# Sorting edges on one core: one-hots and halves of the sort's moves dealt out differently to VectorE and ScalarE, seven matrix-product tiles placed ahead of the first move

## The reference, cut to what matters

```python
def _L0_gnn_ref(vertex_features, edge_index, w0, w1):
    w0_features = vertex_features @ w0
    w1_features = vertex_features @ w1
    dst, src = (edge_index[0], edge_index[1])
    messages = w1_features[src]
    neighbours = jax.ops.segment_sum(messages, dst, num_segments=vertex_features.shape[0])
    return jax.nn.relu(w0_features + neighbours)
...
edge_index = jnp.stack([src, dst])
x = _layernorm(x + _L0_gnn_ref(x, edge_index, L0_gnn_w0, L0_gnn_w1), axis=-1)
x = _layernorm(x + _L1_gnn_ref(x, L1_gnn_W, L1_gnn_attn_src, L1_gnn_attn_dst, edge_index, edge_type_8), axis=-1)
```

## Time and profile before

| | |
|---|---|
| median of 3 runs | 2756.26 us (2753.54 to 2758.73) |
| the profiled execution | 2753.3 us, span 2751.5 us |
| PE busy | 2293.7 us (83%) |
| VectorE busy | 1939.8 us (70%) |
| GpSimd busy | 1849.2 us (67%) |
| ScalarE busy | 1639.8 us (60%) |

### The profile page before, as it was taken

The page is one execution under the profiler, slowest core; times in us unless marked ns, Lnnn a source line. Parts: engine busy times, 40 slices in busy tenths (PEclk is TensorE's granted clock), DMA queues, the critical chain, the costliest instruction groups (busy, mean ns, idle before and its releaser), DMA issues.

```text
span 2751.5 us, 38106 instructions
## 1 busy us (share of the span) xinstructions
PE 2293.7 (83%) x9936; PEld 1659.4 (60%) x9936; DVE 1939.8 (70%) x4273; ACT 1639.8 (60%) x3465; POOL 1849.2 (67%) x1875
## 2 busy tenths in 40 slices
PE   7787798999999999999997677777778777777775
PEld 3455676777777776777764555565556555555541
DVE  8896666555555555555553688888888888888887
ACT  4563564666666666666654566666666666666643
POOL 1002677777777777777753777777777777777745
PEclk9897899999999999999997688888878887888888
DMA  5202355754544444444454544554455445544435
GB/s 153 67 22 90 117 150 137 228 179 151 167 149 153 159 152 161 154 160 143 155 127 163 138 138 138 147 141 138 138 142 146 138 138 148 139 138 138 142 92 159
DMA packets 177777, 387.53 MB, mean 141 GB/s; under 512 B 42669, under 2 KB 106867, under 8 KB 171042
## 3 DMA queue, kind: packets, MB, share of 16 engines
q0 software_dynamic: 83888, 233.09, 30.1%
q1 hardware_dynamic: 86626, 99.05, 12.3%
q10 hardware_dynamic: 7056, 52.99, 4.9%
HBM read 302.96 MB, written 82.03 MB: 140 GB/s over the span
## 4 chain that ended last, share of the span: by engine, by line
PE 49%; DVE 17%; POOL 13%; issue 12%; DMA 6%; DVEq 2%; ACT 1%; SPq 0%; POOLq 0%; ACTq 0%; PEldq 0%
PE ps L1687 21%; PE ps L1804 10%; PE ps L1739 10%; POOL region L1348 7%; POOL region L1303 5%; DVE nodes L895 4%; DMA region<-ha_d,idx_t 3%; PE ps L1787 2%; DVE region L884 2%; DMA region<-y_d,edge_z 2%; PE ps L1656 2%; DVE nodes L777 1%; PE ps L1644 1%; PE ps L1821 1%; DMA ha_d<-region 1%
## 5 line engine op out<-in xcount | busy, mean ns | idle before, releaser
L1303 POOL DMA_INDIRECT region<-y_d,edge_z x856 | 879.1, 1027 | 466.3 <-issue 240.3
L1348 POOL DMA_INDIRECT region<-ha_d,idx_t x880 | 896.0, 1018 | 306.9 <-issue 246.9
L777 DVE TENSOR_TENSOR nodes<-ps,nodes 128x512 f32 x856 | 592.0, 692 | 508.5 <-PE ps L1687 389.4
L1687 PE MATMUL ps<-region 128*128 128x256 f32 x3424 | 802.0, 388 | 66.3 <-DMA region<-y_d,edge_z 36.1
L1687 PEld LDWEIGHTS ps<-region 128*128 128x128 f32 x3424 | 657.8, 194 | 229.0 <-issue 109.3
L1804 PE MATMUL ps<-region 128*128 128x264 f32 x1760 | 618.6, 483 | 123.6 <-DVE nodes L895 119.3
L1804 PEld LDWEIGHTS ps<-region 128*128 128x128 f32 x1760 | 357.1, 229 | 300.0 <-DVE nodes L895 219.8
L895 DVE TENSOR_TENSOR nodes<-ps,nodes 128x264 f32 x880 | 373.5, 424 | 99.0 <-DVE nodes L895 48.6
L1461 ACT ACTIVATE region<-iota_n,edge_z 128x256 f32<-128x256 f32 x856 | 364.7, 499 | 62.7 <-PE ps L1687 56.5
L1739 PE MATMUL ps<-region,edge_z 128*128 128x512 f32 x784 | 359.9, 592 | 5.5 <-ACT region L1503 4.3
L1556 ACT ACTIVATE region<-region,ones 128x512 f32<-128x512 f32 x220 | 158.8, 722 | 270.2 <-PE ps L1804 264.9
(11 more groups left out here) (265 smaller groups left out, 1860.0 us busy)
## 6 DMA issues: line engine op xcount, KB each, us to landing
ha_d<-region ACTq DMA_DIRECT2D x49, 1056.0 KB, 4.8
region<-near_d SPq DMA_DIRECT2D x55, 512.0 KB, 5.4
region<-ha_d,idx_t POOLq DMA_INDIRECT x880, 4.1
region<-y_d,edge_z POOLq DMA_INDIRECT x856
edge_z<-level_d SPq DMA_DIRECT2D x55, 136.0 KB, 4.0
kl_d<-region SPq DMA_DIRECT2D x8, 903.0 KB, 9.8
edge_z<-kl_d SPq DMA_DIRECT2D x55, 129.0 KB
y_d<-edge_z SPq DMA_DIRECT2D x25, 256.0 KB, 3.2
```

What stands on the lines that cost most here:

```text
L777: v.tensor_tensor(into, ps[:, u, :], into, ALU.add).then_inc(added0, 1)
L1303: g.indirect_dma_start(rows0[c % RING][:, u, :], None, y_d, bass.IndirectOffsetOnAxis(ap=y_idx[:, k:k + 1], axis=0), bounds_check=node_bou ...
L1348: g.indirect_dma_start(rows[s][:, k, :], None, ha_rows, bass.IndirectOffsetOnAxis(ap=idx_t[:, B * b + k:B * b + k + 1], axis=0), bounds_ch ...
L1687: mm = t.matmul(ps[:, u, h * D:(h + 1) * D], lhsT=sel0[c % SEL][:, u, h * P:(h + 1) * P], rhs=rows0[c % RING][:, u, :], start=True, stop=True)
```

## The change

DVE now makes all the windows, also those of moves 0, 4, ..., 28, and no longer makes the halves. It makes the column one-hots of even moves only. ACT makes the halves, in eight instructions for each move (2 sides by 4, 104x64 elements each, a Copy with a scale that is read from `sides`), and the column one-hots of odd moves, as two Abs of 104x856 and one Relu of 104x1712. The pairs of buffers for the columns become three: even moves share one, moves 1, 5, 9, ... and 3, 7, 11, ... have one each; `columns_of(k)` on DVE still waits for `settle(k - 2)`. The ACT copy of the window numbers (`w_f`) is gone. Tiles 41 to 47 of y stand between the turning of `q_row` and the first move, with `columns_of(1)` on ACT after the copy of tile 44; tiles 48 and 49 follow moves 3 and 7.

```diff
 # constants and buffers
-    GOES_AT, Q_AT = 35, 40
+    GOES_AT, Q_AT, GAP = 35, 40, 7
-        S_c = [[view16(region, COLS * n + COLS // 2 * s, COLS) for s in range(2)] for n in range(2)]
+        S_both = [view16(region, at, 2, COLS) for at in (0, COLS, 9 * KR)]
+        S_c = [S_both[0], S_both[1], S_both[0], S_both[2]]
...
         def on_scalar(k):
-            return k % 4 == 0
+            return k % 2 == 1
         def y_tile_at(k):
-            return Q_AT + k // 2 + 1 if k % 2 and Q_AT + k // 2 + 1 < NT else None
+            tile = Q_AT + GAP + k // 4 + 1
+            return tile if k % 4 == 3 and tile < NT else None
...
 # VectorE
             places_of(0)
+            windows_of(0)
             for k in range(NBT):
                 values_of(k)
                 if k + 1 < NBT:
                     places_of(k + 1)
-                if k + 1 < NBT and not on_scalar(k + 1):
+                if k + 1 < NBT:
                     windows_of(k + 1)
-                columns_of(k)
-                if k:
-                    halves_of(k - 1)
+                if not on_scalar(k):
+                    columns_of(k)
...
 # ScalarE
+            def columns_of(k):
+                if k >= 5:
+                    a.wait_ge(o_ps, k - 3)
+                for s in range(2):
+                    last = a.activation(S_c[k % 4][0:WW, s, :], iota_h[0:WW, :], ACT.Abs,
+                                        bias=goes_col[0:WW, PP * (2 * k + s):PP * (2 * k + s) + 1], scale=-1.0)
+                last.then_inc(s_near, 1)
+                near_turns[0] += 1
+                a.wait_ge(s_near, near_turns[0])
+                a.activation(S_c[k % 4][0:WW, :, :], S_c[k % 4][0:WW, :, :], ACT.Relu, bias=ones[0:WW, 0:1],
+                             scale=-1.0).then_inc(cols_a, 1)
+
+            def halves_of(k):
+                a.wait_ge(moved, k + 1)
+                if k >= 2:
+                    a.wait_ge(o_ps, k - 1)
+                for s in range(2):
+                    for h in range(SIDES):
+                        last = a.activation(halves[k % 2][0:WW, s, :, h * HC:(h + 1) * HC],
+                                            ps[0:WW, 2 + k % 2, s * 2 * HC:(s + 1) * 2 * HC].rearrange("p (a n) -> p a n", a=2),
+                                            ACT.Copy, scale=sides[0:WW, 2 * k + s, 0, h:h + 1])
+                last.then_inc(halves_made, 1)
+
+            for tile in range(Q_AT + 1, Q_AT + GAP + 1):
+                keep_products(tile)
+                if tile == Q_AT + 4:
+                    columns_of(1)
             for k in range(NBT):
-                ahead = k // 4 * 4 + 4
-                if ahead < NBT:
-                    windows_of(ahead, TBG // 2 * (k % 4), TBG // 2 * (k % 4) + TBG // 2)
+                halves_of(k)
+                if k and k + 1 < NBT and on_scalar(k + 1):
+                    columns_of(k + 1)
                 if y_tile_at(k) is not None:
                     keep_products(y_tile_at(k))
...
 # TensorE
             turn_rows(q_row, 6).then_inc(sort_ps, 1)
+            for tile in range(Q_AT + 1, Q_AT + GAP + 1):
+                products(tile)
```

More of the change, by code:

```diff
@@ L81, in graph_layers @@
     EARLY = 6
-    GOES_AT, Q_AT = 35, 40
+    GOES_AT, Q_AT, GAP = 35, 40, 7
     assert WW <= P and COLS <= KR and OH <= 512 and E <= P * KR and NP_ * 512 < 2 ** 24
     assert WW * HC < HIGH and HIGH * HIGH <= 2 ** 24 and KR < HIGH and NPAIR <= 16
-    assert OH % 4 == 0 and OH <= 512 and NT - 1 - Q_AT <= NBT // 2 and 2 * NBT * PP <= P
+    assert OH % 4 == 0 and OH <= 512 and 0 <= NT - 1 - Q_AT - GAP <= NBT // 4 and 2 * NBT * PP <= P
     def dram(name, shape, dt):
@@ L197, in graph_layers @@
         q_i = view(region, 9 * KR, KR).bitcast(I32)
-        w_f = view(region, 10 * KR, KR)
         masks = [view(region, GA + KR // 2 * t, KR // 2).bitcast(BF16) for t in range(NPAIR)]
@@ L201, in graph_layers @@
         assert GA + NPAIR * KR // 2 <= RW - COLS
-        win = [view16(region, GA, TB, WW)] + [view16(region, GA + TB * WW // 2 * n, TB // 2, WW, 2) for n in range(1, 4)]
+        win = [view16(region, GA + TB * WW // 2 * n, TB // 2, WW, 2) for n in range(4)]
         at = [view16(region, GA + 2 * TB * WW + TB * HC * n, 2, TB // 2, HC, 2) for n in range(3)]
@@ L338, in graph_layers @@
         (pads_set, edges_in, acol_in, w_in, iotas, setup, sort_ps, sort_in, y_ps, y_done, y_kept, bt_made, masked,
-         counted, v_made, goes_made, cells_made, scans, summed, wp_made, split_made, grids_made, at_made, at_filled, win_v, win_a, moved,
+         counted, v_made, goes_made, cells_made, scans, summed, wp_made, split_made, grids_made, at_made, at_filled, win_v, cols_a, moved,
          halves_made, s_near, s_made, o_ps, y_ready, segs0, sel0_near, sel0_made, added0, pool_turns, rows_stored,
@@ L366, in graph_layers @@
         PS = {"counts": 1, "v": 2, "goes": 3, "q": 4, "bucket": 5, "wab": 6}
-        IN = {"v": 2, "goes": 3, "q": 5, "w_f": 6, "bucket": 8, "cells": 8, "wab": 11}
+        IN = {"v": 2, "goes": 3, "q": 5, "bucket": 7, "cells": 7, "wab": 10}
         def in_pairs(eng, first, end, body):
@@ L616, in columns_of @@
                 for s in range(2):
[L617 removed]
+                    v.tensor_scalar(S_c[k % 4][0:WW, s, :], iota_h[0:WW, :], goes_col[0:WW, PP * (2 * k + s):PP * (2 * k + s) + 1],
                                     None, ALU.is_equal).then_inc(s_made, 1)
[L620 to L629 removed]
             places_of(0)
+            windows_of(0)
             for k in range(NBT):
@@ L1421, in _ @@
             a.wait_ge(wp_made, 2)
-            a.copy(w_f, w_i).then_inc(sort_in, 1)
-            a.wait_ge(sort_in, IN["w_f"])
-            def windows_of(k, first, end):
-                if k >= 4 and first == 0:
-                    a.wait_ge(moved, k - 3)
-                to = win[k % 4]
-                for j in range(first, end):
-                    last = a.activation(to[:, j, :], iota_row[:, 0:WW], ACT.Abs, bias=w_f[:, TB * k + j:TB * k + j + 1],
-                                        scale=-1.0)
-                if end == TB:
-                    last.then_inc(s_near, 1)
-                    near_turns[0] += 1
-                    a.wait_ge(s_near, near_turns[0])
-                    a.activation(to, to, ACT.Relu, bias=ones[:, 0:1], scale=-1.0).then_inc(win_a, 1)
@@ L1633, in _ @@
             turn_rows(q_row, 6).then_inc(sort_ps, 1)
+            for tile in range(Q_AT + 1, Q_AT + GAP + 1):
+                products(tile)
             def move(k):
                 t.wait_ge(at_filled, 2 * k + 2)
-                window_ready(t, k)
+                t.wait_ge(win_v, k + 1)
                 if k >= 2:
@@ L1644, in move @@
                     mm = t.matmul(ps[0:WW, 2 + k % 2, j // TBG * 2 * HC:j // TBG * 2 * HC + 2 * HC],
-                                  lhsT=win[k % 4][:, j, :] if on_scalar(k) else win[k % 4][:, j // 2, :, j % 2],
+                                  lhsT=win[k % 4][:, j // 2, :, j % 2],
                                   rhs=at[k % 3][:, :, j // 2, :, j % 2],
@@ L1651, in settle @@
                 t.wait_ge(halves_made, k + 1)
-                t.wait_ge(s_made, 2 * k + 2)
+                columns_ready(t, k)
                 for s in range(2):
@@ L1656, in settle @@
                             mm = t.matmul(ps[:, 4 + h, 0:OH], lhsT=halves[k % 2][0:WW, s, n, :],
-                                          rhs=S_c[k % 2][s][0:WW, h * OH:(h + 1) * OH], start=(k == 0 and s == 0 and n == 0),
+                                          rhs=S_c[k % 4][0:WW, s, h * OH:(h + 1) * OH], start=(k == 0 and s == 0 and n == 0),
                                           stop=(k == NBT - 1 and s == 1 and n == 1))
```

21 lines of the change are left out of this document (4 added, 17 removed).

## The result

| | before | after |
|---|---|---|
| median | 2754.86 us (5 runs) | 2724.6 us (5 runs, 2718.97 to 2729.65) |
| ratio | 1 | 0.9893, 95% interval 0.9874 to 0.9911 |
| profiled execution, its span | 2753.3, 2751.5 | 2729.65, 2727.8 |
| last settle ends | 246.9 us | 219.9 us |

The change made the kernel faster by 29 us, going by the ratio. A second series of the same kernel gave 2723.34 us and a ratio of 0.9895 (0.9878 to 0.9912), so the gain is no accident of five runs. The 1.4 us are another matter. The range was counted from 2756.3 us for the kernel before, whose later medians were 2750.6 to 2753.9, and both ratios times 2756.3 would be 2727, just inside. What has to be explained is the 9 to 11 us between forecast and result.

The account below looks back on a forecast made before the run. VectorE's pace was taken to bound the sort's moves, with ScalarE nearly level after the change. Last settle at about 227 instead of 246.9 us, 20 earlier: 2753.3 becomes 2733.3, plus 3.0 for the median gives 2736 us, range 2726 to 2749.

Parts of the forecast that it names:

- What bounds, and what the moves save is saved: Moves: VectorE sets the pace; their end releases the first gather, so time saved there is saved in the whole.
- VectorE's sum: Moves: 18.3 us of halves and 10.5 of columns removed, 12.6 of windows added, net 16.2 less; a pair 7.06 us.
- The floor: End of the moves: with VectorE never idle, the last settle ends at 218 us at the earliest.
- The halves' price: ScalarE in the moves: a half lasts 0.31 us, starts 0.21 apart; eight cost 1.70 us of the queue.
- The columns' price: ScalarE in odd moves: two Abs and a Relu take 3.55 us; with halves a pair of moves costs 6.95 us.
- The start: Ahead of the moves: first tiles at half clock, move 0 ends at 116 us, 2.9 us later than at full clock.
- one such spell and half of the tail: 2 to 3 us: Clock in the moves: one half-clock spell and half of the tail add 2 to 3 us; last settle at about 227.
- Rival 1: Moves: VectorE's pace holds and the clock stays up; last settle ends at 218 to 221, time 2729 us; chance 0.17.
- 2: ScalarE bounds the moves, halves starting 0.27 to 0.31 us apart: 14 to 24 us later, 2750 to 2760; chance 0.07.
- 3: ScalarE's halves do not overlap, 2.7 to 3.2 us a move: 30 to 45 us later, 2766 to 2781; chance 0.05.
- Rival 4: Half clock through most of the moves, PE's pair of 10.8 us bounds: no gain, 2755 us; chance 0.06.
- 5: Next stage is held by something other than the sort, so the change brings nothing: 2756 us; chance 0.03.

Follow-up runs that it names:

- after_3: The changed kernel with no edit, its third profile: sort 123.4 us, clock over the moves 1.00, span 2727.9 us.
- again: The changed kernel with no edit, profiled again: sort 126.1 us, clock over the moves 0.95, span 2725.0 us.
- ten_halves: The changed kernel with two more ScalarE copies for each move, to an unused place; ratio 0.9968 to the kernel before, 20 us above the changed kernel.
- columns_dve: The changed kernel with all column one-hots on VectorE; ratio 0.9919 to the kernel before, 6.6 us above the changed kernel.

## Why the prediction was wrong, and where it was right

**What bounds, and what the moves save is saved:** right. The first gather starts 27.1 us earlier, and the runs differ by 29.

**VectorE's sum:** right. I had 16.2 us of net work and the pages show 16.7. The halves cost 18.4 when put back (18.3 worked out), the columns 6.6 net of a wait and a longer end. A pair took 7.09 us for 7.06. The floor was 218 us, and the last settle ended at 219.9.

**The halves' price:** right where it counts. Sixteen took 3.38 us, 0.205 from start to start for my 0.21. The duration of one was longer than I said, median 338 ns for 0.31 us (the changed kernel's halves: min, median and max, first and last start):

```profile
L1430 ACT ACTIVATE region<-ps,region x240: 288/338/426, 113.5 to 217.8; 104x64 f16<-104x64 f32 x120
```

By the Trainium skill (ScalarE: Activation LUTs, "What ACT_TABLE_LOAD costs") one would take 186 + 93 + 53 = 332 ns, an estimate from the page's figures; the trace agrees with that duration. It does not agree with the page's overlap of 93 ns, since 338 less 205 is 133. I had the duration too short and the overlap too small, and the two cancel in the start distance, which is what the sum rests on.

**The columns' price:** 3.66 us from the first Abs to the next halves, not 3.55 (198.66 to 202.32). ScalarE's pair took 6.82 us where it ran without waiting, for 6.95, so it was nearly level with VectorE as forecast, and a little better.

**The start:** the order of events was right and the clock term wrong. I had the first tiles at half clock for 7 us, with move 0 ending 2.9 us late, at 116. It ended at 113.4, as in the reckoning at full clock: half speed ended at about 100 us, after 4 us of tiles rather than 7, so it cost tile 41 only, and ScalarE's columns, for which tile 47 waited 1.39 us, hid even that. (This execution also began 1.0 us earlier; *after_3* did not, and its first settle came at the same time.)

**The step that failed** is the one "I add one such spell and half of the tail: 2 to 3 us", with the 2.9 us of the start: 5 to 6 us for the clock, measured 0 in two profiles and about 3 in the third. It came from the rows of the kernel before, where PE's regular pause was 1.51 us, and I carried its clock over by PE's busy share. The runs show the length of the single pause in its place: with pauses of 0.9 us and less the clock was full at 81% busy, and behind pauses of 1.4 us and more it sometimes fell, once after 12 us of which PE was busy for 11.86. In the new steps PE paused for 1.50 us at 135 and 1.41 at 150, then for no more than 1.03 until the last settle (1.66). That the clock stayed up even through the first two was in part luck, as *again* shows, where both brought a fall. Rival 1, which had this case at 2729 with a chance of 0.17, was the one that came.

**The size of the miss** is 11.4 us, in four parts. The last settle was 7.1 us earlier than 227: 5.5 are the clock, and of the other 1.6 the earlier beginning is 1.0. The profiled execution lost 3.4 later. I had added 2.7 for the median over the profiled execution of before, from three runs that happened to lie high (later medians of the kernel before were 2750.6 to 2753.9), and the profiled execution after is 5.05 above its own median: 7.1 - 3.4 + 2.7 + 5.05 = 11.4. So over 6 of the 11.4 us lie in the sort, nearly all of that in the clock, and the last three terms, a net 4.3, are the spread of executions. I read that spread off three runs as 5 us, and it is 9 to 18 in the larger series of the kernel before. The low end of the range was set 3 us under VectorE's floor, with too little for it.

Of the rivals, 2 and 3 on ScalarE's price did not come, but *ten_halves* shows that they were near: 0.41 us more for a move cost 20 us, where queue time alone would be 8. Rival 4 (half clock throughout) and 5 (nothing gained) did not come.

## What to carry to other kernels

Where two engines pass work back and forth, add up each engine's period of the repeated step from start distances, and forecast the later one; here that gave 7.06 for 7.09 us. Ask of TensorE's clock how long its single pauses in a step will be, and not only how busy it is, and remember that at half clock the same work counts for more in a busy share (a settle took 3.03 us instead of 1.63). When a difference between one profile and a median enters a forecast, take the spread of executions from more than three runs, and let the range's end have it on top of the floor.

## What I had not expected of the hardware

- With pauses of PE of at most 0.9 us the granted clock stayed at 1.00 for 114 us, PE 81% busy (*columns_dve*). Each fall to 0.50 in the moves came behind a pause of 1.4 us or more, in all kernels that had falls there, once after 12 us of which PE was busy for 11.86. Not every such pause brings a fall. Four matmuls put into the pause took the mean clock over the moves from 0.80 to 0.99.
- GpSimd took 3.2 us for a comparison of 104x856 f16 with a value for each partition, 7.4 times VectorE's 0.43, and VectorE's multiply of 128x896 beside it took 823 instead of 611 ns.
- Small copies with a scale pointer out of PSUM last 338 ns but start 205 ns apart.
- The gather stage of the changed kernel took 1176.2 us in one execution and 1182.6 in another.
